# Gathers of expert rows in two mixture stages: each tile's four are issued after the four of the tile in front have landed

## What is computed

```python
def _L1_ffn_ref(x, gate_w, w1, w2, w3, ws1, ws2, ws3):
    xt = x.reshape(-1, DIM)
    weights, indices = _gate(xt, gate_w)               # 4 of 16 experts for each token
    c = jnp.zeros((T, N_EXPERTS)).at[jnp.arange(T)[:, None], indices].add(weights)
    h1 = jnp.einsum('td,edi->tei', xt, w1)
    h3 = jnp.einsum('td,edi->tei', xt, w3)
    a = jax.nn.silu(h1) * h3
    y = jnp.einsum('tei,eid,te->td', a, w2, c)
    z = jax.nn.silu(xt @ ws1) * (xt @ ws3) @ ws2       # the shared expert
    return (y + z).reshape(shape)
...
x = x + 0.5 * _L1_ffn_ref(_layernorm(x, axis=-1), ...)   # stage d, and again as stage f
```

## Time and profile before

| what | us |
|---|---|
| median of 3 runs | 4177.82 |
| lowest and highest of them | 4175.79 to 4180.38 |
| the profiled execution's own time | 4176.92 |
| span of its trace (first to last instruction) | 4175.0 |

### The profile page before, as it was taken

How to read it: one execution, slowest core, us unless ns; L and a number is a source line. 1 busy time by engine, 2 the same in 40 slices (tenths; PEclk the granted TensorE clock), 3 DMA queues, 4 the chain that set the end, 5 groups by cost and what they waited for, 6 DMA issues and landing times. The chain is left out here.

```text
span 4175.0 us, 71302 instructions
## 1 busy us (share of the span) xinstructions
PE 3417.6 (82%) x23668; PEld 2585.4 (62%) x23669; DVE 2394.9 (57%) x4826; ACT 2006.2 (48%) x4064; POOL 1204.7 (29%) x1030
## 2 busy tenths in 40 slices
PE   4599948989896479992598799999999999539954
PEld 4499945555554469992498656566666656429943
DVE  4644445656664554435755565765676575485535
ACT  1566624444443166663444265655565565344411
POOL 2154321121110134432364021122022110226565
PEclk6699978999998579995699899999999999759976
DMA  3244220000002144325256300011011000415544
GB/s 125 92 97 101 36 63 6 17 17 27 17 16 85 54 128 87 81 36 146 80 166 179 133 26 19 14 31 32 2 32 32 17 16 6 136 57 166 160 152 129
DMA packets 209043, 294.07 MB, mean 70 GB/s; under 512 B 32992, under 2 KB 170208, under 8 KB 208480
## 3 DMA queue, kind: packets, MB, share of 16 engines
q1 hardware_dynamic: 155744, 176.32, 12.7%
q0 software_dynamic: 52992, 113.82, 11.8%
HBM read 193.20 MB, written 96.86 MB: 69 GB/s over the span
## 5 line engine op out<-in xcount | busy, mean ns | idle before, releaser
L2459 ACT ACTIVATE e_prob<-e_s_ps,e_small 128x512 f32<-128x512 f32 x512 | 346.5, 684 | 174.4 <-PE e_t_ps L2349 91.5
L2595 DVE TENSOR_REDUCE e_small<-e_s_ps 128x2 f32<-128x1024 f32 x256 | 313.0, 1223 | 143.7 <-PE e_s_ps L2336 135.4
L1867 ACT ACTIVATE b_pt<-b_t_ps 128x1024 f32<-128x1024 f32 (+3 forms) x256 | 180.7, 706 | 308.3 <-PE b_t_ps L1799 307.2
L2550 POOL TENSOR_TENSOR e_wide<-e_small,const 128x512 f32<-128x512 f32 x64 | 66.5, 1039 | 778.6 <-DVE e_small L2684 778.6
L2349 PE MATMUL e_t_ps<-const,e_prob 128*128 128x128 f32 x2048 | 270.6, 274 | 11.4 <-ACT e_pt L2448 6.1
L2370 PE MATMUL e_z_ps<-e_pt,e_v 128*64 128x512 f32 x1024 | 275.5, 617 | 0.4 <-DVE e_zf L2691 0.4
L2349 PEld LDWEIGHTS e_t_ps<-const,e_prob 128*128 128x128 f32 x2048 | 235.0, 141 | 59.1 <-issue 24.2
L2050 DVE TENSOR_REDUCE b_small<-b_s_ps 128x2 f32<-128x1024 f32 (+3 forms) x256 | 209.7, 819 | 85.0 <-PE b_s_ps L1778 80.9
L2601 DVE COPY e_pt<-e_t_ps 128x512 f32<-128x512 f32 x256 | 175.3, 685 | 68.2 <-PE e_t_ps L2349 64.4
L692 DVE TENSOR_TENSOR ce_h_lo<-ce_hid,ce_h_hi 128x512 fp32r<-128x512 f32 x128 | 88.6, 692 | 206.9 <-ACT ce_h_hi L639 185.3
L692 DVE TENSOR_TENSOR ae_h_lo<-ae_hid,ae_h_hi 128x512 fp32r<-128x512 f32 x128 | 88.7, 693 | 206.0 <-ACT ae_h_hi L639 184.0
(11 more groups left out here) (779 smaller groups left out, 11225.9 us busy)
## 6 DMA issues: line engine op xcount, KB each, us to landing
o_rows_dram<-d_big SPq DMA_DIRECT2D x36, 512.0 KB
o_rows_dram<-f_big SPq DMA_DIRECT2D x36, 512.0 KB
ae_raw<-w_dram SPq DMA_DIRECT2D x16, 1024.0 KB
ce_raw<-w_dram SPq DMA_DIRECT2D x16, 1024.0 KB
d_big<-x_dram SPq DMA_DIRECT2D x16, 512.0 KB, 9.2
f_big<-x_dram SPq DMA_DIRECT2D x16, 512.0 KB, 8.8
d_raw<-m_dram SPq DMA_DIRECT2D x54, 128.0 KB, 3.5
f_raw<-m_dram SPq DMA_DIRECT2D x54, 128.0 KB, 3.3
```

Of the source, the lines that this page charges most:

```text
L1867: act.activation(pt[:, kt % 2, a, :, 0:width], t_ps[:, :, 0:width], ACT.Exp).then_inc(p_ready, 1)
L2459: act.activation(prob[:, at], s_ps[:, at], ACT.Exp, bias=nmx[:, at:at + 1], accum_out=sums[:, buf, h * QT + s:h * QT + s + 1]).then_inc(p_ ...
L2595: dve.tensor_reduce(nmx[:, at:at + 2], s_ps[:, at:at + 2], AX.X, ALU.max, negate=True).then_inc(mx_ready, 1)
```

## The change

In `moe`, in POOL's list, the gathers of every tile but the first wait for one more semaphore: that all four gathers of the tile in front have landed.

```diff
             for t in range(here * GT):
                 if t >= TAKE:
                     gp.wait_ge(used, t - TAKE + 1)
+                if t:
+
+                    gp.wait_ge(taken[(t - 1) % TAKE], 16 * TOPK * ((t - 1) // TAKE + 1))
                 for k in range(TOPK):
                     gp.indirect_dma_start(out=takes[:, t % TAKE, k], out_offset=None, in_=o_rows,
                                           in_offset=bass.IndirectOffsetOnAxis(ap=back[:, t, k:k + 1], axis=0)).then_inc(taken[t % TAKE], 16)
```

## The result

The changed kernel takes 4233.62 us, the median of four runs (4224.73 to 4235.65). The kernel before, on the same chip, took 4176.81 (4172.32 to 4180.38). The ratio is 1.0138 [1.0125, 1.0151], 56.8 us more. The forecast was 4211.4, in a range of 4198 to 4244: the sign and the mechanism came out, the size by 22 us too small.

A forecast was written before the change was run, and what follows sets the result against it. Bound: POOL's gather issuing at stage f's end, then one landing, additions and store. From 3973.13, adding 156.5 issuing, 62.0 pauses, 1.84 + 2.04 + 4.45 tail and 8.6 transfers gives span 4208.6; plus 2.8, 4211.4 us, range 4198 to 4244.

The forecast's parts named there:

- The likeliest case: Stage f's end: POOL pauses for each tile's landing, its waits for DVE go; span 4208.6, time 4211.4 us, chance 0.64.
- Issuing: Stage f: POOL issues four gathers and three gaps a tile, 4.89 us, 32 times, 156.5 us.
- third rival: Stage f: additions and gathers, released together, hold each other up; 31 us more, a time of 4242 us, chance 0.04.
- Pauses: Stage f: POOL waits 2.0 us for landing between two tiles, 31 times, 62.0 us.
- Other transfers: Stage f: SP's loads and stores delay landings, 2.1 us at the start and five times 1.3, 8.6 us.
- The tail: After POOL's last gather: 1.84 us to the additions, 2.04 of additions, 4.45 to the end of the span.
- What is taken away: Stage f: POOL's 27.7 us of waits for DVE were counted as gone.
- The cover: Stage f: tile 8, due at 4030, needs tile 0's additions, over at 4022.8 before the change, so POOL need not wait.
- first rival: Stage f: quiet between tiles is too short, waits for DVE stay; 26.3 us more, a time of 4238, chance 0.26.
- Stage d: Three waits among 16 gathers, put at nothing because the shared expert holds the additions; without that cover 5 us.
- second rival: Stage f: not slower, since pauses below 1.19 us cost less than the waits they replace; 4172.7 or 4164 us, chance 0.04.

The follow-up runs named there:

- used_early: The changed kernel with POOL's wait for DVE's count of used tiles moved to the fourth gather of the tile in front; 4214.84 us, ratio 1.0097.
- gap_long: The kernel before, with POOL clearing 1024 unused words a partition between two tiles' gathers, no wait for landing; 4168.57 us, ratio 0.9984.
- half_rows: The kernel before, with each end gather of the mixture stages moving 512 bytes of a row, not 1024; 4173.1 us, ratio 0.9990.

## Why the prediction was right, and where its size was off

The likeliest case came true, with a span 22.0 us above its 4208.6: the mechanism was right, and the terms of the sum were too small. Term by term, in the profiled execution:

**Issuing**: 156.5 forecast; 132.8 + 30.4 = 163.2 measured, 6.7 more. Of it 1.1 is one gap at 4196 us (1.42 in place of 0.30), and the gathers have 5.1, since their mean rose from 998 to 1038 ns. This is the third rival's mechanism at a sixth of its price: a gather that starts beside DVE's additions takes 1.19 where it took 0.95, and each of the eight beside DVE's L1439 took 1.46. The sum took the mean of before, when additions and gathers met by chance: 29 gathers over 1.0 us, now 38. The same rival also weighed that POOL could be held for all 2.04 us of a tile's additions, and found that the mean of the rows disagrees. The 2.04 are four instructions of 0.48 in one row (x4), and POOL is held for what is left of one of them: the last section has the rows.

**Pauses**: 62.0 forecast. Seven tiles with one wait at 2.04 and 24 with two at 2.56 give 75.7, so 13.7 more. The value for one wait, chosen between 1.84 and 2.1, was right. The step that failed is the assumption that the wait for `used`, already met, costs nothing behind a pause; used_early shows it.

**Other transfers**: 8.6 forecast. The six long pauses have 14.8 us above the plain ones, 6.2 more. They are 4.80, 4.79, 5.34, 6.29, 3.84 and 4.03; I had put 2.1 on the first and 1.3 on each other, and it was 2.8 on the first and 2.4 on the others. I had argued that a bunch meets a landing with its tail only. The trace does not bear this out: the packets of SP's bunch ahead of tile 9 (1.57 MB) ran from 4032.24 to 4038.87. They began while tile 8's gathers were being issued (4029.86 to 4034.81) and lasted 4.1 us beyond, so the whole landing met them, not their tail. The bunches of 1.57 MB (tiles 9 and 13) cost 2.8 and 3.7 us, those of 1.05 MB (tiles 5, 17, 21) 2.8, 1.3 and 1.5. No run tested this term by itself.

**The tail**: 1.84 + 2.04 + 4.45 forecast. The last gather starts at 4221.32 and takes 0.95, the additions start 1.88 later and take 2.05, and the span ends 4.40 after: 8.33 both times.

**What is taken away**: counted as gone, and gone. The cover held, with tile 8's pause ended by the landing and not by DVE. The **first rival** had the nearest number, 4238, and was wrong: POOL has no wait for DVE left. Its number came near by the sum of other things. It asked whether a quiet of 1.8 us a tile is enough for PE, ACT and DVE; gap_long shows that 1.13 us between two gathers a tile is.

**Stage d**: put at nothing; it gave 8.6 us back against the one trace of before, some 6 over all traces. The cover that I named, the shared expert, was itself held up by the stalls, so ending them shortened it. The 5 us that the later gathers might cost were hidden, as expected, and the stretch got shorter by the stalls. The text had allowed "a few either way" and then counted none.

**The second rival** fell with the first pause: none is under 2.01.

From first gather to the end of the span: 163.2 + 90.5 + 8.3 = 262.0 measured, 235.4 forecast, 26.6 more. The first gather came 4.5 us earlier than in the kernel before, from D's 8.6 less and some 4.1 of drift the other way in stages that the change does not touch (stage d's first gather alone came 4.8 later, at 2286.72). 26.6 - 4.5 is the 22; so a gain that I had not counted hid part of what the sum lacked.

## What to carry to other kernels

A wait on a transfer just issued costs the whole way there and back, here 2.0 us, each time, on an engine that only issues; if the wanted effect is a pause, try shorter and rarer ones (here 1 us per tile did as much for PE as the full wait, and the landing at each fourth tile, which only shortened the stalls, is in the fastest kernel). A wait already met is free on an engine that runs ahead and cost half a microsecond behind another wait, so put it on an earlier instruction. When one engine may hold another, read a row xN as N instructions before you price the hold. And when engines that share no data with a stream of gathers slow down, ask what ends the slowdown: the time that it hides in may be in another stage than the one you look at.

## What the runs showed of the hardware

**While POOL issues gathers back to back for long, the other engines start their instructions one by one.** In the kernel before it begins some 17 us after the first gather (16 to 20 in the other traces that have it) and ends some 4 us behind the last of the first 32 (4013.60 to 4018). It depends neither on the bytes (half_rows) nor on a wait for landing (gap_long); a gap of 1.13 us after each fourth gather prevents it, one of 0.49 does not. PE in order of time, half_rows:

```profile
3997.34 0.59 PE L60 MATMUL f_ph<-f_xh,f_zw_hi 128*128 128x512 f32 x1 [1.73 <-issue]
3999.44 0.58 PE L61 MATMUL f_ph<-f_xl,f_zw_hi 128*128 128x512 f32 x1 [1.51 <-issue]
4000.84 0.59 PE L62 MATMUL f_ph<-f_xh,f_zw_lo 128*128 128x512 f32 x1 [0.82 <-issue]
4002.95 0.59 PE L60 MATMUL f_ph<-f_xh,f_zw_hi 128*128 128x512 f32 x1 [1.52 <-issue]
4005.75 0.59 PE L61 MATMUL f_ph<-f_xl,f_zw_hi 128*128 128x512 f32 x1 [2.21 <-issue]
4008.54 0.58 PE L62 MATMUL f_ph<-f_xh,f_zw_lo 128*128 128x512 f32 x1 [2.21 <-issue]
```

And in the kernel before:

```profile
4005.47 0.59 PE L60 MATMUL f_ph<-f_xh,f_zw_hi 128*128 128x512 f32 x1 [2.43 <-issue]
4006.88 0.59 PE L61 MATMUL f_ph<-f_xl,f_zw_hi 128*128 128x512 f32 x1 [0.81 <-issue]
4008.97 0.58 PE L62 MATMUL f_ph<-f_xh,f_zw_lo 128*128 128x512 f32 x1 [1.51 <-issue]
4011.07 0.59 PE L60 MATMUL f_ph<-f_xh,f_zw_hi 128*128 128x512 f32 x1 [1.52 <-issue]
```

The starts are 2.10, 1.40, 2.11, 2.80 and 2.79 us apart in the first, and 1.41, 2.09 and 2.10 in the second, all multiples of 0.70 within 0.02, with half the bytes and with all. What sets this step, and by what way POOL's gathers reach the other engines, stays open: no run kept POOL as busy without issuing gathers. The Trainium skill, "Runtime: NRT & Kernel Launch", section "Instruction fetch mechanics", has instruction blocks fetched by a DMA queue of the engine's own. The page of the kernel before has two such queues, with 307 packets in the whole span:

```profile
q8 instruction: 172, 2.82, 0.3%
q14 instruction: 135, 1.11, 0.1%
```

From 3990 to 4018 us, the stalled stretch, it has none of their packets under way, only the gathers':

```profile
## 3 DMA queue, kind: packets, MB, share of 16 engines
q0 software_dynamic: 952, 2.59, 31.9%
```

so PE was not waiting for a long fetch; whether it was refilled in another way these rows can't tell.

**A gather that starts beside a DVE operation with two inputs in SBUF is held until that one operation ends.** A gather of the changed kernel's stage f takes 0.95 us, that at 4040.16 took 1.19 and that at 4042.91 took 1.46. DVE's row at 4039.51 is four additions; the second of them, by itself, is this:

```profile
4040.03 0.48 DVE L1468 SCALAR_TENSOR_TENSOR f_big<-f_w_hi,f_small,f_big 128x256 f32<-128x256 f32 x1
```

It ends at 4040.51, 0.35 us after the gather has begun, and L1439 ends at 4043.54, 0.63 us after its gather has begun. The extra times, 0.24 and 0.51, are each some 0.12 less than that. It is so throughout: in the traces of all 14 kernels 387 gathers of stage f took over 1.0 us, and each ended 0.82 to 0.84 us after the end of such an operation that was under way when it began. The operations of DVE with one input in PSUM (L1416, L1435, L1457) held none: 24 gathers of the changed kernel began beside only these, and none took over 1.0 us. The Trainium skill, "SBUF — State Buffer", section "Who interferes with whom", has a DVE instruction with two inputs in SBUF contend with a GpSimd instruction that reads SBUF, over ports that are locked for one of them. The trace agrees, one instruction at a time: 0.24 and 0.51 us, not the 2.05 of four additions.
